# Routed Fourier filter on one core: the per-image rounds put into slot-by-channel layout, with paired half-array products

## The reference, cut to what matters

```python
xp = star_scale * jnp.square(jax.nn.relu(xp)) + star_bias          # xp = x @ w_pw1, 256 channels
xf = jnp.fft.rfft2(xp, axes=(1, 2), norm='ortho')
weight = jnp.einsum('bfc,hwf->bhwc', routeing.astype(cw.dtype), cw)
spatial_weight = jnp.einsum('bfc,hwf->bhwc', spatial_routeing, spatial_weights)
xs = jnp.fft.irfft2(xf * weight, s=(H, W), axes=(1, 2), norm='ortho')
out = xp * spatial_weight + xs
out = jnp.einsum('bhwm,dm->bhwd', out, w_pw2)                      # back to 128 channels
```

## Time and profile before

| what | value |
|---|---|
| median of 3 runs | 262.82 us (262.64 to 263.25) |
| profiled execution: its own time, its span | 262.2 us, 260.4 us |
| TensorE matmul busy | 240.2 us (92%) |
| TensorE weight load busy | 186.8 us (72%) |
| VectorE busy | 194.9 us (75%) |
| ScalarE busy | 160.6 us (62%) |
| GpSimd busy | 110.1 us (42%) |
| chain that ended last | 66% TensorE, 12% VectorE, 9% issue, 5% GpSimd, 4% ScalarE |

### The profile page before, as it was taken

How to read it: one execution, slowest core, us unless ns; L and a number is a source line. 1 busy time by engine, 2 the same in 40 slices (tenths; PEclk the granted TensorE clock), 3 DMA queues, 4 the chain that set the end, 5 groups by cost and what they waited for, 6 DMA issues and landing times.

```text
span 260.4 us, 6938 instructions
## 1 busy us (share of the span) xinstructions
PE 240.2 (92%) x2225; PEld 186.8 (72%) x2225; DVE 194.9 (75%) x548; ACT 160.6 (62%) x378; POOL 110.1 (42%) x198
## 2 busy tenths in 40 slices
PE   0687799998999999999999999999999999999983
PEld 0677665554545555886988988988888889889873
DVE  3998999955929626996779998668678678677672
ACT  2024486656775748655775776775775766766741
POOL 2422341110000002257445656746647657657582
PEclk9999999999999999999999999999999999999999
DMA  7999200000000000001000010010100100100101
GB/s 214 358 319 330 116 3 3 1 4 3 0 3 0 3 0 3 1 23 43 11 32 20 23 42 24 30 33 20 36 27 20 40 20 20 40 20 20 40 29 52
DMA packets 9482, 13.18 MB, mean 51 GB/s; under 512 B 732, under 2 KB 8924, under 8 KB 9332
## 3 DMA queue, kind: packets, MB, share of 16 engines
q1 hardware_dynamic: 9428, 12.80, 15.2%
q10 hardware_dynamic: 32, 0.08, 0.2%
HBM read 8.69 MB, written 4.19 MB: 49 GB/s over the span
## 4 chain that ended last, share of the span: by engine, by line
PE 66%; DVE 12%; issue 9%; POOL 5%; ACT 4%; DMA 3%; SPq 1%; POOLq 0%; ACTq 0%; DVEq 0%
PE bank L1156 19%; PE bank L1317 9%; PE bank L1263 7%; PE bank L1329 7%; PE bank L1250 6%; PE bank L1336 4%; PE bank L1066 4%; DMA x_all<-in_x 3%; PE bank L1292 2%; POOL prod L412 2%; PE bank L1221 1%; PE bank L1171 1%; PE bank L1096 1%; DVE stats L702 1%; PE bank L1306 1%
## 5 line engine op out<-in xcount | busy, mean ns | idle before, releaser
L411 POOL TENSOR_TENSOR prod<-t_re,t_im 128x256 f32<-128x256 f32 x32 | 23.3, 729 | 52.4 <-DVE t_re L983 52.0
L964 DVE TENSOR_SCALAR xp<-sq_v,later_sb 128x512 f32<-128x512 f32 x32 | 17.6, 550 | 32.3 <-ACT sq_v L574 32.0
L1156 PE MATMUL bank<-z_all,split_h 128*64 128x450 f16 (+2 forms) x320 | 37.4, 374 | 1.8 <-ACT z_all L489 1.8
L1317 PE MATMUL bank<-later_sb,prod 128*128 128x128 f32 x256 | 36.4, 285 | 1.1 <-POOL prod L412 1.1
L421 POOL TENSOR_TENSOR waves<-folded 128x128 f32<-128x128 f32 x31 | 14.1, 456 | 50.9 <-DVE eo L971 50.7
L1317 PEld LDWEIGHTS bank<-later_sb,prod 128*128 128x128 f32 x256 | 31.1, 192 | 5.3 <-POOL prod L412 3.7
L1263 PE MATMUL bank<-later_sb,eo 128*128 128x128 f32 x256 | 34.0, 276 | 0.4 <-DVE eo L970 0.4
L604 ACT ACTIVATE folded<-bank,coef 128x128 f32<-128x128 f32 x32 | 11.8, 367 | 34.5 <-PE bank L1336 28.2
L1329 PE MATMUL bank<-qt,later_sb 128*128 128x256 f32 x128 | 32.9, 380 | 0.0
L1263 PEld LDWEIGHTS bank<-later_sb,eo 128*128 128x128 f32 x256 | 31.1, 192 | 1.4 <-DVE eo L970 0.7
L1156 PEld LDWEIGHTS bank<-z_all,split_h 128*64 128x64 f16 x320 | 17.2, 110 | 16.8 <-issue 3.1
(11 more groups left out here) (162 smaller groups left out, 484.3 us busy)
## 6 DMA issues: line engine op xcount, KB each, us to landing
x_all<-in_x SPq DMA_DIRECT2D x8, 512.0 KB, 8.9
out<-x_all SPq DMA_DIRECT2D x32, 128.0 KB, 1.7
sp_t<-in_branch_s SPq DMA_DIRECT2D x1, 2560.0 KB, 15.3
later_sb<-in_later SPq DMA_DIRECT2D x1, 918.5 KB, 8.9
sym_all<-in_sym SPq DMA_DIRECT2D x1, 292.5 KB
early_sb<-in_early SPq DMA_DIRECT2D x1, 278.0 KB, 3.7
rwf_t<-in_branch_r SPq DMA_DIRECT2D x1, 256.0 KB, 12.4
kan_sb<-in_kan ACTq DMA_DIRECT2D x1, 80.8 KB, 3.3
```

Source lines behind the costliest of these rows:

```text
L411: pool.tensor_tensor(prod[:, :, :, 0, :], halved[0][:, :, 0], halved[1][:, :, 1], ALU.subtract).then_inc(prod_ready, 1)
L1156: last = mm(dst[:, :, rows_out, cols_out], w[:, t, :], pixels(z_all[:, b:b + 2, part, :])[:, :, rows_in, cols_in], start=(n == 0 and t in ...
L1317: last = mm(bank[1][:, odd * C:(odd + 1) * C], prod[:, m, odd].rearrange("p a s -> p (a s)"), pw2_t[:, m, :], start=(m == 0), stop=(m == 1))
```

## The change

- The transform has its operands exchanged: `forward` (64 slots) is now the stationary operand and `eo` (256 middle channels) the moving one. Each product fills 64 output rows; the even and the odd half go to partitions 0 to 63 and 64 to 127 of the same bank. The spectrum is slot by channel.
- `mix` has its operands exchanged too, so that the mixed filters are slot by channel and pixel by channel.
- The inverse is done before the second product `w_pw2`, on 256 channels: 4 products of 64 rows, even slots into bank 1, odd slots into half of bank 7 (`inverse_waves`).
- The tables are changed so that the two real frequencies of a slot need no special case: `terms` has two operations in place of three, and a third plane of `spec` (a copy times a sign) is written by ScalarE.
- VectorE adds the even waves (`even_waves`) and the odd waves with both signs (`odd_waves`) to the spatial term. TensorE transposes the sum (`turn_pixels`, now on `u_px`, behind the inverse), ScalarE copies it (`by_channel`), and one product with `w_pw2` follows (`second_wide`). `reduce`, `compose`, `y_copy`, `folded_copy`, `spatial_mix` and `unfold` are gone.
- ScalarE does the affine step (`affine`), GpSimd the sum and the difference (`halves`) and the gate times the image (`scale_image`). `finish` adds the bias and writes the final image.
- In a round, TensorE's order is now `waves_of(i+1)`, `mix(i+1)`, `inverse_waves(i)`, `turn_route`, `turn_pixels(i-1)`, `expand(i+3)`, `second_wide(i-1)`. `expand` runs one image further ahead. More rounds are written out in place of looped.
- Before the rounds, `expand(1)` now stands ahead of `waves_of(0)`.

```diff
             def products(i):
-                pool.wait_ge(terms_ready, 3 * i + 3)
+                pool.wait_ge(terms_ready, 2 * i + 2)
                 if not isinstance(i, int) or i >= 1:
-                    pool.wait_ge(y_done, i)
...
+                    pool.wait_ge(inv_done, i)
+                pool.tensor_tensor(prod[:, 0, :], t_re[:, 0, :], t_im[:, 1, :], ALU.add).then_inc(prod_ready, 1)
+                pool.tensor_tensor(prod[:, 1, :], t_re[:, 1, :], t_im[:, 0, :], ALU.add).then_inc(prod_ready, 1)
+
+            def halves(i, p):
+
+                pool.wait_ge(xp_ready, i + 1)
                 if not isinstance(i, int) or i >= 1:
-                    pool.wait_ge(fin_ready, i)
...
+                    pool.wait_ge(dft_done, i)
+                pool.tensor_tensor(eo[:, 0, :], xp[p][:, 0, :], xp[p][:, 1, :], ALU.add).then_inc(eo_ready, 1)
+                pool.tensor_tensor(eo[:, 1, :], xp[p][:, 0, :], xp[p][:, 1, :], ALU.subtract).then_inc(eo_ready, 1)
+
+            def scale_image(i):
+
+                pool.tensor_tensor(one(x_all, i), one(x_all, i), one(coef[:, 0, :].unsqueeze(2), i).broadcast_to([P, HW]),
+                                   ALU.mult).then_inc(x_scaled, 1)
...
+            def affine(i, p):
+
+                act.wait_ge(sq_ready, i + 1)
+                if not isinstance(i, int) or i >= 2:
+                    act.wait_ge(qt_ready, i - 1)
+                act.activation(xp[p].rearrange("p t m -> p (t m)"), sq_v, ACT.Identity,
+                               bias=star[:, 1:2], scale=star[:, 0:1]).then_inc(xp_ready, 1)
+
             def spectrum(i):
                 act.wait_ge(dft_done, i + 1)
...
+                act.activation(spec[:, 0:2, :].rearrange("p a m -> p (a m)"), bank[2], ACT.Identity).then_inc(spec_ready, 1)
+                act.activation(spec[:, 2, :], bank[2][:, MED:2 * MED], ACT.Identity, scale=sign).then_inc(spec_ready, 1)
...
+            def by_channel(i):
+                act.wait_ge(xt_done, i + 1)
...
+                    act.wait_ge(sp_done, i)
+                act.activation(u_ch.rearrange("p m s -> p (m s)"), bank[5], ACT.Identity).then_inc(ut_ready, 1)
...
+                for a, (product, parts) in enumerate(((t_re, spec[:, 0:2, :]), (t_im, spec[:, 0:3:2, :]))):
+                    dve.wait_ge(spec_ready, 2 * i + 1 + a)
+                    tt(product, parts, mixed_slot[:, a, :].unsqueeze(1).broadcast_to([P, 2, MED]), ALU.mult).then_inc(terms_ready, 1)
+
+            def spatial(i, p):
+                dve.wait_ge(w_done, i + 1)
+                dve.wait_ge(xp_ready, i + 1)
+                tt(qt[p], xp[p], mixed_pixel, ALU.mult).then_inc(qt_ready, 1)
+
+            def even_waves(i, p):
+                dve.wait_ge(inv_done, i + 1)
+                dve.wait_ge(qt_ready, i + 1)
+                tt(qt[p], qt[p], wave_even.unsqueeze(1).broadcast_to([P, 2, MED]), ALU.add).then_inc(q_even_ready, 1)
+
+            def odd_waves(i, p):
+                dve.wait_ge(q_even_ready, i + 1)
                 if not isinstance(i, int) or i >= 1:
-                    dve.wait_ge(sp_done, i)
...
+                    dve.wait_ge(xt_done, i)
+                for t, op in enumerate((ALU.add, ALU.subtract)):
+                    tt(u_px[:, t, :], qt[p][:, t, :], wave_odd, op).then_inc(u_ready, 1)
...
+                for part in range(2):
+                    for odd in range(2):
+                        last = mm(bank[2][64 * odd:64 * odd + 64, part * MED:(part + 1) * MED], forward[:, odd, part, :], eo[:, odd, :],
                                   start=True, stop=True)
                 last.then_inc(dft_done, 1)
...
+            def inverse_waves(i):
+
+                pe.wait_ge(prod_ready, 2 * i + 2)
+                if not isinstance(i, int) or i >= 1:
+                    pe.wait_ge(u_ready, 2 * i)
+                for part in range(2):
+                    for odd, dst in enumerate((wave_even, wave_odd)):
+                        rows_o = slice(64 * odd, 64 * odd + 64)
+                        last = mm(dst, inverse[rows_o, part, :], prod[rows_o, part, :], start=(part == 0), stop=(part == 1))
+                last.then_inc(inv_done, 1)
...
+            def second_wide(i, turned_routes):
+
+                pe.wait_ge(ut_ready, i + 1)
+                pe.wait_ge(rt_out, turned_routes)
...
+                    pe.wait_ge(fin_ready, i)
                 for m in range(2):
-                    last = mm(bank[6][:, 0:HW], pw2_t[:, m, :], qt[:, m, :], start=(m == 0), stop=(m == 1))
+                    last = mm(bank[6][:, 0:HW], pw2_t[:, m, :], u_ch[:, m, :], start=(m == 0), stop=(m == 1))
                 last.then_inc(sp_done, 1)
...
             def round_of(i, pair, j, half=0, between=None):
...
+                inverse_waves(i)
+                if j == 0 and (not fixed or i + 2 < NB):
+                    turn_route(pair + 1, half)
+                if not fixed or i >= 1:
+                    turn_pixels(i - 1)
+                if not fixed or i + 3 < NB:
...
+                    expand(i + 3)
+                if not fixed or i >= 1:
+                    second_wide(i - 1, min(pair + 2, NB // 2) if fixed else pair + 2)
```

359 lines of the change are left out of this document (134 added, 225 removed).

## The result

The kernel after the change takes 270.74 us (median of 4 runs, 270.4 to 274.09), beside 262.73 us for the kernel before in the same measurement. The ratio is 1.0326, with a 95% interval of 1.0281 to 1.037. The forecast was 265.5 us, slower, from the wait for `by_channel`. The sign and that wait are right, the size is not: 8.0 us in place of 2.7. The profiled execution has a span of 268.8 us and took 270.63 us.

A forecast was written before the change was run, and what follows sets the result against it. TensorE was taken to set the pace. Start -1.4, rounds +1.2, end +0.6 and +2.3 sum to +2.7 us: 262.2 becomes 264.9, plus 0.6 for the median, given as 265.5 us; range 257.5 to 271.5.

The forecast's parts named there:

- The slots of a round: TensorE's blocks in one round, without waits: 4.47 us, with half a turn_route 4.52 us.
- Side by side: In waves_of and inverse_waves the halves run in pairs: each block is 4 steps of 0.216 us, not 8.
- E: Rival: the pairs don't run side by side in the new shapes; 1.7 us more a round, 317 us; 5%.
- The new wait: TensorE's second_wide waits for ScalarE's by_channel: 0.97 us against a cover of 0.76, so TensorE stands 0.21 us a round.
- case A: The forecast itself: the wait for by_channel takes what the pairing gives; 262 to 268.5 us; 50%.
- the term for the rounds: The steady rounds: 4.83 us each in place of 4.79, 30 x 0.04 = +1.2 us.
- case C: Rival: by_channel starts later; with 0.2 us more the round is 5.03 us and the time 271.5 us; 19%.
- This ring has room: Chain mix, terms, products, inverse_waves: products end 4.5 us into the round, inverse_waves wants them at 6.1.
- the start's gain: Before the rounds: VectorE's terms(0) can start earlier and mix(1) comes at about 101.95, 1.4 us gained.
- The end: Last rounds: 0.6 us lost as expand lies inside the wait, 2.3 us lost from mix(31) to the last sum's end.
- The clock: TensorE's clock: granted in full, 2.4 GHz, in every slice before the change, so no term came from it.
- D: Rival: a full drain of TensorE at each change of shape; 0.28 us more a round, 274 us; 4%.

The follow-up runs named there:

- e2: The changed kernel with turn_pixels(i-1) ahead of inverse_waves(i) on TensorE, and by_channel ahead of route_copy on ScalarE; 264.35 us.
- e8: The changed kernel with both products of each pair in the same half of the array, the odd half of the spectrum left out of the result; 320.36 us.
- e1: The changed kernel with ScalarE's copy by_channel split into two copies of 256 columns, second_wide's first product waiting for the first half alone; 264.26 us.
- e3: The changed kernel with TensorE's 12 looped rounds written out in plain code, in the same order; 269.19 us.
- e5: The changed kernel with turn_route right behind mix, then turn_pixels(i-1), then inverse_waves(i); ScalarE keeps route_copy ahead of by_channel; 262.95 us.
- e7: The changed kernel with e5's and e6's orders, e3's written rounds, later second logits, spatial(31) behind odd_waves(30), last by_channel in halves; 262.13 us, again 262.06 us.
- e9: e7 with the second half's window sums, image sums, logits, softmax and parts moved one or two rounds later; 260.67 us, again 260.79 us.
- e6: The changed kernel with spatial(i+1) ahead of even_waves(i) on VectorE; 270.85 us.
- e11: The kernel before the change with only the second half's routing moved two rounds later; 262.38 us, ratio 0.9981.
- e4: The changed kernel with the products of waves_of and inverse_waves reordered, so that neighbours in the program share a half of the array; 271.33 us.

## Why the prediction was right in kind and wrong in size

**The slots of a round: right.** In the odd rounds every block is within 0.03 us of its forecast, and e2's round without a wait is 4.62 us where the sum of slots said 4.47. Most of the 0.15 lies in the transposes, which with a change of shape on both sides take 0.58 us (e2, 208.23 to 208.81) where 0.49 was put; 0.03 more is `waves_of`.

**Side by side: right.** e8 takes it away and a round grows by 1.71 us; E had put 1.7 on its absence, and E fell.

**The new wait: right, and the seat of the loss in the rounds.** e1 halves the copy and e2 moves it under the inverse. They take 6.5 and 6.4 us off the 270.7. The pairing's gain is real and the wait takes it, which was case A.

**What failed first: the term for the rounds, 30 x 0.04 = +1.2 us.** It was worked out for one steady round and multiplied by 30. An undisturbed pair of rounds is 4.81 and 4.94 us after, 4.71 and 4.87 before: 0.085 us a round and not 0.04. (The blocks added up to 0.03 us too much for the odd round before, and to 0.03 too little for the one after.) That `mix(7)` to `mix(15)` came out as forecast (+0.34, forecast +0.32) is luck: there the kernel before has three rounds of 4.95 us beside the routing, and the changed kernel has none above 4.94. In the fifteen rounds from `mix(15)` it was +2.61 in place of +0.6: 1.2 us for fifteen steady rounds, and 1.4 because six even rounds there take 5.17 us in place of 4.94. Of these 0.23 us a round, 0.16 is the late issue on TensorE that e3 removes. The other 0.07 is on ScalarE, whose own loop stands in both kernels. In the loop the route's copy starts 0.12 us behind the route's last product (207.67 to 207.79), in all written rounds from `mix(7)` on 0.04. `by_channel` stands behind it and starts 0.08 us late; in e3's rounds of 5.01 us it does the same (0.11 us behind the last transpose, 0.04 in its rounds of 4.94). So case C, the late copy, was there with under half of its 0.2 us, in every second round of a loop only.

**What failed most: the first six rounds, +2.75 us in place of +0.24.** The step was "This ring has room", with the other engines costed for a steady round. There the room is real: the odd rounds of e2, e5, e7 and e9 take 4.61 to 4.62 us, which is TensorE's own work. But between `mix(1)` and `mix(7)` VectorE also has the sums for the routing. There it is full (5.93 of 6 us from 108 to 114). It was also near full before (5.84), but then it had been busy 5.28 of the 6 us from 102 on; now it is 4.02, with the 1.98 us for `spectrum(1)` in it. So the start's gain, -1.27 us and forecast well, was made on TensorE, and VectorE got a third of it: `terms(1)` starts at 104.87 (before 105.28), and `terms(3)` at 116.07 (before 115.88). In the round of the logits, TensorE then waits for `finish`, the last in VectorE's queue, where before the same block began 0.32 us behind `mix` without a wait:
```profile
119.75 1.93 PE L1202 MATMUL bank<-sp_t,win_p 128*32 128x256 f32 x32 [0.39 <-DVE x_all L986]
```
That is 0.78 us behind `mix(4)` at 118.97, 0.46 more than before. What supports the account: e6 changes the order and gains nothing, and e9 moves the sums and gains 1.6 us. e11 moves them in the kernel before, where VectorE hadn't idled, and gains 0.35. That `spectrum(1)`'s place in ScalarE's queue is the root is argued from the timeline; a kernel with it ahead of `affine(2)` was not run. The prediction did look at that queue, for `spectrum(0)`, and stopped one image too soon.

**A second share of the first rounds: VectorE's small operations got longer.** The timeline of `windows(1)` in the changed kernel, with GpSimd's `halves`:
```profile
108.34 0.74 POOL L424 TENSOR_TENSOR eo<-xp 128x256 f32<-128x256 f32 x1
108.41 0.70 DVE L863 TENSOR_TENSOR win<-win,cols_sum 128x8 f32<-128x8 f32 x1
...
109.04 0.73 POOL L425 TENSOR_TENSOR eo<-xp 128x256 f32<-128x256 f32 x1
109.10 0.78 DVE L866 TENSOR_TENSOR bars<-rows,corners 128x8 f32<-128x8 f32 x2
...
114.65 0.70 DVE L912 TENSOR_SCALAR win_p<-win 64x8 f32<-64x8 f32 x1
```
VectorE's first two groups take 0.15 and 0.24 us in the kernel before, at 108.30 and 108.46, where no GpSimd operation runs (one other of the group met one there too, with 0.61 us). Here each begins just behind one of GpSimd's and lasts until that one ends (108.41 + 0.70 = 109.11, 108.34 + 0.74 = 109.08). `windows(1)` takes 2.30 us from its start to the next `terms`, where before it took 1.52 to the next affine step. `image_sums(1)` (the last line) has two operations of one input that met `halves` too, with 0.70 and 0.65 us for 0.17, and takes 2.40 us in place of 2.08; before, one of its operations met `products`, with 0.66. Together that is 1.1 us more of VectorE's time. The Trainium skill (GPSIMD Engine Reference, 1. Specifications) says that GpSimd shares its SBUF interfaces with VectorE, with contention when VectorE's operation is in a two-port mode or has two inputs in SBUF, as those of `windows(1)` have; the trace agrees, with 0.70 us for 0.15. The prediction costed GpSimd's new work as hidden, because GpSimd has time. That it holds up VectorE, at the place where VectorE is full, was not in it. No run moved `halves` back, so its share of the 2.75 us is not measured by itself. In e9 `windows(1)` is free of it and 1.0 us shorter than in e7, so up to 1.0 us of e9's 1.6 can be this, and not the peak.

ScalarE's price for `affine` was wrong too, 812 ns for 630, and that for the third plane of `spec`, which is multiplied by a column (L596, 467 ns for 380). The groups of the changed kernel by line (busy us, mean ns of one):
```profile
L588 ACT ACTIVATE xp<-sq_v,later_sb 128x512 f32<-128x512 f32 x32 | 26.0, 812 | 2.7 <-DVE qt L969 1.2
L581 ACT ACTIVATE sq_v<-relu_v 128x512 f32<-128x512 f32 x32 | 20.2, 630 | 1.1
```
Both read and write 128x512 f32 in on-chip memory. What differs is the function and that the bias and the scale are a column each. That is 182 ns more. In a steady round it costs nothing, as e5's rounds of 4.61 us without a wait show; in the stretch from 102 to 108 it stands ahead of `spectrum`.

**The end: right in its chain.** +0.73 and +2.63 us for 0.6 and 2.3. The 0.61 us more behind the last sum had no term, and the change isn't needed for it: e1, e2, e3, e5 and the kernels from e7 on have the 2.3 us of the kernel before there. The changed kernel (2.93), e4 (3.31) and e6 (3.15) have more, and in these three a 16 KB packet of the instruction queue is under way while the last image is stored (in the changed kernel from 266.34 on, for 0.89 us). That this packet holds up the store was not tested.

**The clock: not a term.** It fell to 1.2 GHz at 108 in the profiled execution, and `mix(2)` to `mix(3)` took 6.53 us there. But where it didn't fall (e2, e5) `mix(3)` to `mix(4)` took 5.7 in place of 4.94, waiting for VectorE, and `mix(4)` was only 0.4 us earlier. By `mix(7)` nothing is left of it: e4, without the fall, is at 34.83 us behind `mix(1)`, the changed kernel at 34.91. Four runs of the changed kernel have clocks of 0.993 to 1.0; those of 0.993, 0.999 and 1.0 have spans of 268.8, 268.6 and 269.0 us.

**Changes of shape, D: fell.** The last pass of L1308 in the first round shown ends at 203.87 + 1.13 = 205.00 us, and L1241 starts at 204.93, before it. The Trainium skill (TensorEngine Tiling (Array Packing), Key Properties) has a change of mode drain the engine. Here a change costs 0.1 us, from the last start of L1308 at 204.62 to 204.93, 0.31 in place of 0.216; D had 0.38. The next mode's first pass starts 0.07 us before the last record of the one before ends, but the ends are modelled, so this speaks against D's price and doesn't show what the engine does in between.

## What to carry to other kernels

A wait that hides in the sum of a round can often be bought off by order alone: here the same work, with the copied block moved ahead of a long one, went from 3.3% slower to level with the kernel before, and to 0.5 to 0.6% faster once another engine's peak was moved to later rounds. Cost the first rounds, the looped rounds and the last ones each for itself: a steady round times the count missed 4.5 us of this 8.4. A loop can make waits late on the engine that is the bound and on the one it waits for. When a change brings one engine's start forward, look whether the engine that is full next can start earlier too; if it can't, the gain is not one; and work given to GpSimd is only free where VectorE has time to wait for it.

## What the runs showed of the hardware that was not expected

- Products that use different halves of TensorE's array ran side by side even where their neighbours in the program shared a half: 1.09 us for 8 passes of 128x64 in e4, against 1.94 us when all of them sat in one half (e8).
- A matmul block behind waits whose counts depend on a loop's register was issued 0.21 us behind the copy that it waited for, against 0.05 in the other round of the same loop and 0.04 with the loop written out (e3). Where other work covers it, as in e5, it costs nothing. ScalarE's route copy started 0.12 us behind its product in a loop, and 0.04 us in written rounds.
- VectorE's operations on 128x8 took 0.70 us in place of 0.15 where they met a GpSimd operation on 128x256, and those of one input on 64x8 took 0.65 to 0.70 in place of 0.17.
- TensorE's clock stood at 1.2 GHz from about 108 to 111.6 us after stretches in which the engine was busy 54% and 74% of the time; the eight passes of `inverse_waves` then took 2.06 us instead of 1.13, and the total time didn't change. In e4, busy 59% and 74% of the same stretches, it stayed at 2.4 GHz.
